# The row of reciprocals in node order, and a later request for the next adjacency

## The reference

```
v, q, k = tanh(h @ wv + bv), tanh(h @ wq + bq), tanh(h @ wk + bk)      # 512 x 128
scores  = q @ k.T                                                        # 512 x 512
att     = softmax(scores * mask - NEG * (1 - mask), axis=2)              # mask is adj
return att @ v                                                           # 512 x 128
```

## Time and profile before

| | us |
|---|---|
| three runs | 877.64, 874.22, 877.91; median 877.64 |
| the profiled execution | 871.59, of which 869.70 are the span |
| PE busy | 754.4 (87%) |
| DVE busy | 572.3 (66%) |
| ACT busy | 428.4 (49%) |
| POOL busy | 357.0 (41%) |
| DMA, mean rate | 36 GB/s |
| granted TensorE clock, mean | 0.971 |

### The profile page before, as it was taken

The page is one execution under the profiler, slowest core; times in us unless marked ns, Lnnn a source line. Parts: engine busy times, 40 slices in busy tenths (PEclk is TensorE's granted clock), DMA queues, the critical chain, the costliest instruction groups (busy, mean ns, idle before and its releaser), DMA issues.

```text
span 869.7 us, 11347 instructions
## 1 busy us (share of the span) xinstructions
PE 754.4 (87%) x3680; PEld 526.5 (61%) x3680; DVE 572.3 (66%) x1631; ACT 428.4 (49%) x897; POOL 357.0 (41%) x475
## 2 busy tenths in 40 slices
PE   3649799898989899898989899898989899898754
PEld 2426567665756667665756667665766667665433
DVE  3266668677676768677677768677677768674432
ACT  2024645637374645637364645627364645725220
POOL 3133534545362534545362534545362534542200
PEclk9769999999999999999999999999999999999996
DMA  6100110202020120203020120202020120000010
GB/s 164 47 0 13 19 62 6 68 12 73 13 74 14 18 69 4 70 13 74 12 74 13 22 64 2 71 13 74 13 74 13 20 66 1 19 13 19 14 18 7
DMA packets 38491, 31.22 MB, mean 36 GB/s; under 512 B 24608, under 2 KB 26144, under 8 KB 38432
## 3 DMA queue, kind: packets, MB, share of 16 engines
q1 hardware_dynamic: 38432, 30.49, 14.3%
HBM read 28.32 MB, written 2.16 MB: 35 GB/s over the span
## 4 chain that ended last, share of the span: by engine, by line
PE 50%; issue 17%; POOL 15%; DVE 11%; ACT 4%; DMA 1%; POOLq 0%; SPq 0%; DVEq 0%
PE turn_ps L1068 12%; PE pre_ps L957 8%; PE post_ps L957 4%; POOL rstd_pre L433 4%; PE pre_ps L974 3%; PE turn_ps L1060 3%; POOL k_lo L505 2%; PE pre_ps L920 2%; DVE h_nat_pre L724 2%; POOL centred_pre L436 2%; PE qkv_ps L1011 2%; DVE score_ps L810 2%; DVE h_nat_pre L716 2%; PE qkv_ps L1016 2%; PE post_ps L1083 2%
## 5 line engine op out<-in xcount | busy, mean ns | idle before, releaser
L608 ACT ACTIVATE negz<-negz,negmax 128x512 f32<-128x512 f32 x128 | 92.3, 721 | 69.4 <-DVE negmax L818 69.4
L433 POOL TENSOR_TENSOR rstd_post<-vareps_post,nhalf 128x4 f32<-128x4 f32 x32 | 32.8, 1024 | 222.1 <-DVE vareps_post L706 222.1
L1068 PE MATMUL turn_ps<-pt,v_n 128*128 128x512 f32 x256 | 116.2, 596 | 0.7 <-ACT pt L615 0.7
L567 ACT ACTIVATE y_t_pre<-pre_ps 128x512 f32<-128x512 f32 x48 | 28.7, 597 | 148.0 <-PE pre_ps L957 148.0
L810 DVE TENSOR_TENSOR score_ps<-score_ps,a_nat 128x512 f32<-128x512 f32 x128 | 89.0, 696 | 16.4 <-PE score_ps L1046 15.5
L957 PE MATMUL pre_ps<-at_hi,u_pair_pre 128*128 128x512 f32 x192 | 87.6, 456 | 7.2 <-DVE u_pair_pre L746 5.2
L818 DVE CUSTOM_DVE_ANT_0 negz<-score_ps,gate 128x512 f32<-128x512 f32 x128 | 88.5, 692 | 4.4
L433 POOL TENSOR_TENSOR rstd_pre<-vareps_pre,nhalf 128x4 f32<-128x4 f32 x32 | 33.9, 1059 | 128.7 <-DVE vareps_pre L706 128.7
L615 ACT ACTIVATE pt<-turn_ps 128x512 f32<-128x512 f32 x128 | 74.0, 592 | 17.8 <-PE turn_ps L1060 15.7
L1060 PEld LDWEIGHTS turn_ps<-ident,negz 128*128 128x128 f32 x512 | 60.8, 140 | 32.4 <-issue 15.8
L957 PE MATMUL pre_ps<-at_lo,u_pair_pre 128*128 128x512 f32 x192 | 78.5, 409 | 0.0
(11 more groups left out here) (135 smaller groups left out, 1732.3 us busy)
## 6 DMA issues: line engine op xcount, KB each, us to landing
a_nat<-in_adj SPq DMA_DIRECT2D x16, 1024.0 KB, 8.4
inv_row<-inv_d SPq DMA_DIRECT2D x32, 256.0 KB, 4.0
x_in<-in_x SPq DMA_DIRECT2D x16, 128.0 KB, 6.1
out<-x_out SPq DMA_DIRECT2D x16, 128.0 KB, 1.9
inv_d<-inv_total SPq DMA_DIRECT2D x32, 2.0 KB, 1.4
cheb_ws<-in_L_gnn_weight SPq DMA_DIRECT2D x2, 64.0 KB, 4.8
att_w<-in_L_gnn_a_wv SPq DMA_DIRECT2D x2, 64.0 KB, 2.5
att_w<-in_L_gnn_a_wk SPq DMA_DIRECT2D x2, 64.0 KB, 2.3
```

The costliest lines, as they stand in the source:

```text
L433: gp.tensor_tensor(rstd[t][:], vareps[t][:], nhalf[:, 0:RB], ALU.pow)\
L608: sc.activation(probs[:, i, :], negz[:, i, :], ACT.Exp, bias=negmax[:, i:i + 1], scale=-1.0, accum_out=total[:, i:i + 1]).then_inc(probs_d ...
L1068: mm = te.matmul(turn_ps[0][:], v_n[a][:, j * P:(j + 1) * P], pt[:, j, :], start=(j == 0), stop=(j == RB - 1))
```

## The change

`inv_d` becomes one line of 512 floats in the order of the nodes. L380 writes element (p, i) of `inv_total` to place 128 i + p, so that neighbours along a partition's four numbers are 512 bytes apart in DRAM. L385 reads the line as it is. The multiplication in `attend` then reads all three operands without a step. In SP's loop a wait for `inv_spread` of the spread just issued stands ahead of the load of graph n+3.

```diff
-        inv_d = nc.dram_tensor("inv_d", [P, RB], F32)
+        inv_d = nc.dram_tensor("inv_d", [N], F32)
...
-                sp.dma_start(inv_d[:], inv_total[:]).then_inc(inv_sent, 16)
+                sp.dma_start(inv_d.rearrange("(i p) -> p i", p=P), inv_total[:],
+                             allow_slow_non_contiguous=True).then_inc(inv_sent, 16)
                 sp.wait_ge(inv_sent, 16 * (2 * g.n + a + 1))
...
-                sp.dma_start(inv_row[:], inv_d.rearrange("p i -> (p i)").partition_broadcast(P))\
+                sp.dma_start(inv_row[:], inv_d[:].partition_broadcast(P))\
                     .then_inc(inv_spread, 16)
...
                 spread(Graph(0, n), 1)
                 if n + SLOTS < B:
+                    sp.wait_ge(inv_spread, 16 * (2 * n + 2))
                     load(Graph(0, n + SLOTS))
...
-                ve.tensor_tensor(to[:].rearrange("h (i p) -> h i p", p=P),
-                                 turn_ps[0][:].rearrange("h (i p) -> h i p", p=P),
-                                 inv_row[:].rearrange("h (p i) -> h i p", i=RB),
-                                 ALU.mult).then_inc(attended, 1)
+                ve.tensor_tensor(to[:], turn_ps[0][:], inv_row[:], ALU.mult).then_inc(attended, 1)
```

## The result

The changed kernel takes 1142.54 us (1140.02 to 1144.58, 4 runs) against 875.93 for the kernel before (872.89 to 877.91): 1.305 times as long, 95% interval 1.299 to 1.310. The forecast was 872.9 us, the range 868.5 to 879. It went the way of rival A, the slow scattered send, and far beyond the price put on it there.

What follows compares the result with a forecast made beforehand. PE waiting behind DVE's second-layer L832 was taken as the bound. Terms: -4.5 (full rounds) - 0.8 (last two rounds) + 0.6 (send) = -4.7 us, from 877.64 to 872.9 us; range 868.5 to 879.

Steps and rivals of the forecast that it cites:

- rival A: Scattered send (L380) slow, its wait replacing the stride; +11 us at 4.0 us; chance 0.13 over 3.3 us, 0.11 for 2.2-3.3.
- L380 as a scatter: The send as 512 pieces of 4 B lands in 1.7 us instead of 1.4; +0.6 us in the last two rounds.
- w: Landing time of the scattered send in us, by which the slow-send rival was priced; 1.4 for the old send.
- Its own rule: Send of w costs 2 (w - 1.4) in the last two rounds, plus w - 3.2 in 14 first-layer spreads beyond 3.2.
- the break-even: Send length at which the slow send's cost equals the 5.3 us gained: w = 3.3; below it a smaller gain.
- L832 of the second layer: Multiplication in attend, on the path once a round; shortened, it gives PE's scores2 0.30 us, 15 times, 4.5 us.
- 0.69 us for the instruction: L832 without the step takes 0.69 us instead of 1075 ns, saving 0.385 us each, 32 times.
- the cover of the first layer: In the first layer the send may take 1.8 us longer, 3.2 in all, with the row's 4.0, without PE waiting.
- the load's wait at zero: SP's wait ahead of the load delays it about 4 us, with 32 us of cover: 0, bounds 0 either side.
- the second layer's cover: Room for a slow send before the second layer's attend: 2.0 us, raised to 3.9 by the load's wait.

Runs made afterwards that it cites:

- e12: The changed kernel unaltered, run once more as the measure for the idle-matmul run: 1099.51 us, ratio 1.258 to the kernel before.
- e13: Changed kernel plus idle PE matmuls, 20 before the second layer's wait for attended, 14 before the wait in scores2: 1034.72 us, ratio 1.185.
- e11: Changed kernel, but the send is 256 pieces of 8 B over the same 2 KB: 874.98 us, kernel before beside it 871.77.
- e14: Changed kernel, but the 512 sent words lie 8 bytes apart in DRAM and the row is read from x: 874.83 us.
- e15: Kernel before plus load's wait; ACT orders the second layer's row for a step-free multiplication, except in the last graph: 870.67 us, ratio 0.9966.
- e1: Kernel before with only the multiplication without a step; old send, order and load: 869.64 us, ratio 0.9949.
- e2: Kernel before with only the wait ahead of the load added: 873.77 us, ratio 1.0008.
- e5: The changed kernel unaltered, once more, on the same chip as the run without the load's wait: 1099.21 us, ratio 1.259.
- e6: Changed kernel without the wait ahead of the load: 1120.77 us, ratio 1.283 to the kernel before.
- e4: Changed kernel, but each sent float goes to its own 64-byte line in DRAM and the row is read from x: 864.28 us.
- e10: Changed kernel, but only the first of each partition's four reciprocals is sent, 128 words, and the row is read from x: 1041.10 us.
- e8: Kernel before plus load's wait; ACT copies the second layer's row into node order, DVE multiplies there without a step: 872.58 us, ratio 0.9979.

## Why the prediction was wrong

**The step that failed** is the term "L380 as a scatter". It took 1.7 us for the send, between 1.4 and 1.9, +0.3 us; measured were 8.1 to 9.1. The working took the packet's time (8.7 ns) and a store of 512 pieces of 256 B as its near rows. Both are silent on what happened. The DMA view of the changed kernel, 507.1 to 517.1 us in 40 slices of 0.25 us (busy share in tenths), for the send issued at 507.17:

```profile
DMA  9100810000900000000000000000000000000000
```

The first digits are the store of x_out, the 8 and 1 at 508.1 are the scatter's packets, the single 9 is one packet of another queue. The same view from 507.9 to 508.7 counts the send's 528 packets; by 508.6 the engines are done, and the landing comes at 516.1: what takes 7.5 us is no packet's time. The store's pieces are 256 B each and the send's old ones 16 B. The new form, single words side by side, was outside what any row measured, in just the respect that the text itself named (rival A). It left the upper end open ("4 or more") and then cut the range at 879, with 0.13 for everything above. A term without an upper bound, which comes twice in each round, should have widened the range far more.

The Trainium skill, "DMA: Bandwidth & Descriptors", section "Specifications", with its read-modify-write below 512 B, pointed the right way. By it all three forms would pay, and the traces have them far apart: 16 B pieces land in 1.4 us, words 64 B apart in 2.1, crowded words in 9.1.

**Rival A's mechanism was right, its size too small.** It was priced at w = 4.0, +11 us. Its own rule, put to the measured send, gives for the changed kernel: send 9.5 and row 5.0, 14.5 in all, against the 3.2 + 4.0 = 7.2 that the first layer covers and the 5.3 + 4.0 = 9.3 of the second, 7.3 + 5.2 = 12.5 us a round, x 14 = 175; in the last two rounds 29.0 against the 12.4 of before, 17; less 5.3: +187. Measured were +267. For e12 the same (8.6 and 4.6) gives 14 x 9.9 + 14 - 5.3 = +147, measured +227. Both times 80 us are missing. The idle matmuls take back 65 of them and bring e13 to +162. So the covers were right within some 15 us in 150, and what is missing beside them is mostly the granted clock, which the forecast didn't have at all: it asked what a wait costs, and not what PE's speed is after it. The trace of before had it, in the last two rounds, where the chain runs from the row's landing through L832 into the pair of matmuls that take 1.02 us elsewhere:

```profile
812.88 2.00 PE qkv_ps L1011 x2
```

**The price under the break-even** is less sure than the forecast had it. Rival A's rule gives a gain of 2.1 us for a send of 3.0, but e11 took 874.98 against 871.77, and e14, with 3.5 and a shorter row, 874.83 against 872.65. Behind their 14 rounds e11 takes 88.7 us and e14 85.7, where the kernel before takes 81.9, at a granted clock of 0.76 and 0.80 over the last 82 us in place of 0.86. e15 with the old send shows 86.7 and 0.78 as well, so single executions don't tell how much of that is the send.

**Right:** that L832 of the second layer bounds the round, and by 0.30 us (e1: 48.66 us, as forecast; 4.1 us measured in all, 5.3 forecast, inside the interval 2.8 to 6.0); 0.69 us for the instruction; the cover of the first layer, up to 7.2 us of send and row, for most rounds (e11 and e14, 6.8 each, lose 1.0 and 3.1 us in 14 rounds against e1); the load's wait at zero in the covered regime (e2). **Named, but not priced:** that this wait raises the second layer's cover from 2.0 to 3.9 us. Over 14 rounds that makes 27 us with a slow send, and 21.6 were measured (e5, e6), against the bounds of 0 on either side. **Open:** e4, one run, is 9.4 us under the kernel before. Its row is read from x and lands in 3.2 us. In the profiled executions its 14 rounds are 4.2 us shorter, and what comes behind them 3.8 (78.1 against 81.9); how much of that second part is the shorter row isn't shown.

## What to carry to other kernels

Before moving a permutation from an engine to a DMA, count the pieces and see how closely they will lie in DRAM: a write of single floats side by side took 8 to 9 us here where the same bytes in 16 B pieces took 1.4, and no packet time showed it. A term without an upper row must not be closed by the nearest one; its end of the range stays open. And where a new wait can empty TensorE's queue for microseconds in each round, add what the lower clock costs behind it (here 65 of 227 us).

## What the runs showed of the hardware

- 4 B pieces to DRAM: 512 of them land in 2.1 us at a distance of 64 B (e4) and in 8 to 9 us side by side; 128 side by side take 7.2 (e10). The 528 packets of one crowded send pass between 507.9 and 508.7 us, and it lands at 516.1.
- A row read from DRAM that follows a crowded send lands later too: 4.6 to 5.0 us in the changed kernel, 3.8 in e2, which has the old send and the same wait ahead of the load. It isn't that the row was just written: a row from x takes 4.5 behind the crowded send of e10 and 3.2 behind the spaced one of e4.
- A step of 16 B in an SBUF source of 512 floats costs DVE 0.38 us (1075 against 692 ns). ACT's copy with that step takes 1117 ns (e8, median), against 592 for its copies of the same size without one (L615), which read from PSUM.
- Measured three times (the result, e5, e12), the send of one program landed in 9.1, 8.2 and 8.1 us, and the kernel took 1142.5, 1099.2 and 1099.5 us.
- TensorE's granted clock was 1.00 up to 541 us and 0.50 from 547 to 550, behind 6.8 us without a matmul; the pair of L1010 then took 2.08 us in place of 1.02.
